# Cross-attention on one core: weighted context with the context as the moving operand, turned back by PE

## What is computed

```python
q = jnp.einsum('bte,ef->btf', emb, Wq) + bq
k = jnp.einsum('bml,le->bme', latent, Wk) + bk
v = jnp.einsum('bml,le->bme', latent, Wv) + bv
w = jnp.einsum('bte,bme->btm', q, k) * scale
w = jax.nn.softmax(w, axis=1)
pred = jnp.einsum('btm,bme->bte', w, v)
x = pred + emb
mu = jnp.mean(x, axis=-1, keepdims=True)
var = jnp.var(x, axis=-1, keepdims=True)
return (x - mu) * jax.lax.rsqrt(var + EPS) * gamma + beta
```

## Time and profile before

| | us |
|---|---|
| median of 3 runs (151.82 to 151.93) | 151.87 |
| the profiled execution | 151.6 |
| its span | 149.8 |

### The profile page before, as it was taken

The page is one execution under the profiler, slowest core; times in us unless marked ns, Lnnn a source line. Parts: engine busy times, 40 slices in busy tenths (PEclk is TensorE's granted clock), DMA queues, the critical chain, the costliest instruction groups (busy, mean ns, idle before and its releaser), DMA issues.

```text
span 149.8 us, 3112 instructions
## 1 busy us (share of the span) xinstructions
PE 138.9 (93%) x1070; PEld 130.7 (87%) x1070; DVE 119.8 (80%) x227; ACT 85.8 (57%) x292; POOL 87.5 (58%) x78
## 2 busy tenths in 40 slices
PE   7899999899899999999999999999999999999900
PEld 7789999798898989999998989899998989897700
DVE  0799989699777888779697978779697968777981
ACT  4468365289527937575573938475573938474410
POOL 0350049809032495866849494856749494859880
PEclk9999999999999999999999999999999999999996
DMA  4999659998065579889888989999888984653123
GB/s 136 296 352 418 275 154 285 377 293 322 25 209 198 193 285 334 288 267 306 265 263 305 267 321 280 322 257 335 263 260 284 285 308 122 241 190 114 55 69 95
DMA packets 11336, 37.14 MB, mean 248 GB/s; under 512 B 1422, under 2 KB 1934, under 8 KB 11322
## 3 DMA queue, kind: packets, MB, share of 16 engines
q1 hardware_dynamic: 9714, 34.50, 69.1%
q10 hardware_dynamic: 1608, 2.46, 4.6%
HBM read 33.68 MB, written 3.28 MB: 247 GB/s over the span
## 4 chain that ended last, share of the span: by engine, by line
PE 70%; DVE 14%; POOL 6%; DMA 3%; issue 2%; ACT 1%; SPq 1%; POOLq 1%; DVEq 0%
PE ps_U L372 27%; PE ps_S L358 26%; PE ps_Y L391 12%; DVE xu L624 6%; PE ps_U L333 3%; POOL result L810 3%; DMA wkT<-WkT 3%; DVE xT_lo L612 2%; POOL resid L800 2%; DVE wq_lo L598 2%; DVE wkq L604 1%; DVE W_lo L708 1%; PE ps_w L381 1%; POOL prob L790 1%; ACT xu_hi L483 1%
## 5 line engine op out<-in xcount | busy, mean ns | idle before, releaser
L494 ACT ACTIVATE expo<-scores,negmax 121x100 f32<-121x100 f32 x96 | 35.0, 366 | 26.6 <-DVE negmax L644 26.6
L358 PE MATMUL ps_S<-G,ctxT_in 128*121 128x100 f32 (+1 forms) x384 | 43.7, 270 | 0.6 <-DVE scores L640 0.6
L372 PEld LDWEIGHTS ps_U<-prob,ctx_in 121*128 121x128 f32 x360 | 42.4, 192 | 1.5
L358 PEld LDWEIGHTS ps_S<-G,ctxT_in 128*121 128x121 f32 (+1 forms) x384 | 41.9, 185 | 0.9 <-issue 0.9
L372 PE MATMUL ps_U<-prob,ctx_in 121*128 121x100 f32 x360 | 42.4, 274 | 0.0
L804 POOL TENSOR_TENSOR rstd<-vareps,neg_half 100x1 f32<-100x1 f32 x16 | 15.4, 960 | 27.5 <-DVE vareps L680 25.5
L790 POOL TENSOR_TENSOR prob<-expo,rinv 121x600 f32<-121x600 f32 x16 | 19.0, 1189 | 9.0 <-DVE rinv L651 9.0
L800 POOL TENSOR_TENSOR resid<-x_in,bvw 100x512 f32<-100x512 f32 x16 | 20.4, 1273 | 4.6 <-ACT bvw L511 4.4
L640 DVE TENSOR_TENSOR scores<-ps_S,c_rows 121x600 f32<-121x600 f32 x16 | 12.5, 782 | 13.2 <-issue 11.8
L657 DVE TENSOR_REDUCE probsum<-prob 121x100 f32<-121x600 f32 x16 | 19.8, 1239 | 1.0 <-POOL prob L790 0.6
L810 POOL TENSOR_TENSOR result<-scaled,beta_rows 100x512 f32<-100x512 f32 x15 | 19.3, 1291 | 0.0
(11 more groups left out here) (92 smaller groups left out, 184.1 us busy)
## 6 DMA issues: line engine op xcount, KB each, us to landing
ctx_in<-ctx SPq DMA_DIRECT2D x16, 768.0 KB, 6.4
ctxT_in<-ctxT SPq DMA_DIRECT2D x16, 722.0 KB, 6.6
xT_in<-xT SPq DMA_DIRECT2D x8, 400.0 KB, 5.9
x_in<-x SPq DMA_DIRECT2D x16, 200.0 KB
out<-result ACTq DMA_DIRECT2D x12, 200.0 KB
wqT<-WqT SPq DMA_DIRECT2D x4, 256.0 KB, 3.4
out<-result SPq DMA_DIRECT2D x3, 200.0 KB
wkT<-WkT SPq DMA_DIRECT2D x4, 128.0 KB, 3.9
```

What stands on the lines that cost most here:

```text
L358: last = nc.tensor.matmul(ps_scores(c)[0:rows(c), :], ctxT_in[:, q, l * M + c * MP:l * M + c * MP + rows(c)], G[:, l, bass.ds(b * T, T)], ...
L372: last = nc.tensor.matmul(ps_U[:, q, l * T:(l + 1) * T], ctx_in[0:rows(c), q, c, l * P:(l + 1) * P], prob[0:rows(c), q, c * T:(c + 1) * T] ...
L494: last = nc.scalar.activation(expo[0:MP, q, c * T:(c + 1) * T], scores[0:MP, q, c * T:(c + 1) * T], ACT.Exp, bias=negmax[0:MP, q, c:c + 1] ...
```

## The change

- `weighted_ctx` swaps its operands: `prob` of a chunk (100 columns) is stationary and the chunk's 256 context columns move. Six matmuls take the place of twelve, and the result has the query in the partition.
- Since the next step needs the context column there, ACT copies the result to `UT` (`take_UT`), and PE turns it with two transposes into `ps_c` (`turn_U`); `upper_U` and `lower_U` read `ps_c`.
- In a turn, the matmuls of the scores of batch b and of the weighted context of batch b-2 alternate: score half 0, weighted, score half 1, for each chunk. Both sets of waits stand ahead of the first matmul (`scores_and_weighted`).
- The values of batch b-3 follow that block, then the turning of batch b-2.
- `ctx_in` has three buffers; the order of SP's queue stays as it is. `centred` and `scaled` lie in the space of `wqT`.
- The turns of ACT, DVE and POOL are in another order, and the last batch is no longer split by halves. `identity` is made by POOL at the start.

The core of the diff:

```diff
-        ctx_in = sb("ctx_in", [P, 2, MC, L])
+        ctx_in = sb("ctx_in", [P, NC, MC, L])
...
+        identity = sb("identity", [T, T])
+        UT = sb("UT", [T, 2, L])
...
-            def next_ctx(b, q):
-                sp.wait_ge(U_done, b - 1)
-                load_ctx(b, q)
+            def next_ctx(b):
+                if b >= NC:
+                    sp.wait_ge(U_done, b - NC + 1)
+                load_ctx(b)
...
+            def before_weighted(b, q):
+                pe.wait_ge(ctx_loaded[b % NC], 16 * (b // NC) + 16)
+                pe.wait_ge(prob_set, b + 1)
+                if not first_two(b):
+                    pe.wait_ge(UT_set, b - 1)
+                else:
+                    pe.wait_ge(G_set, NG)
+
+            def weighted_chunk(b, q, c):
+                done = nc.tensor.matmul(ps_U[0:T, q, 0:L], prob[0:rows(c), q, c * T:(c + 1) * T],
+                                        ctx_in[0:rows(c), b % NC, c, :], start=(c == 0), stop=(c == MC - 1))
+                if c == MC - 1:
+                    done.then_inc(U_done, 1)
...
+            def scores_and_weighted(b, q, between):
+
+                before_scores(b, q)
+                before_weighted(b - 2, q)
+                for c in range(MC):
+                    score_chunk(b, q, c, 0)
+                    weighted_chunk(b - 2, q, c)
+                    score_chunk(b, q, c, 1)
+                    if c == 1 and between is not None:
+                        between()
+
+            def turn_U(b, q):
+                pe.wait_ge(UT_set, b + 1)
+                if b > 0:
+                    pe.wait_ge(Uhi_set, b)
+                    pe.wait_ge(Ulo_set, b)
                 else:
-                    pe.wait_ge(G_set, NG)
+                    pe.wait_ge(identity_set, 2)
+                    pe.wait_ge(c_set, NG)
                 for l in range(LC):
-                    for c in range(MC):
-                        last = nc.tensor.matmul(ps_U[:, q, l * T:(l + 1) * T],
-                                                ctx_in[0:rows(c), q, c, l * P:(l + 1) * P],
-                                                prob[0:rows(c), q, c * T:(c + 1) * T], start=(c == 0), stop=(c == MC - 1))
-                last.then_inc(U_done, 1)
+                    last = nc.tensor.transpose(ps_c[:, l * T:(l + 1) * T], UT[:, q, l * P:(l + 1) * P], identity[:, :])
+                last.then_inc(U_turned, 1)
...
             def turn(b, q):
-                if exists(b):
-                    scores_of(b, q)
-                if exists(b - 3):
-                    values(b - 3, 1 - q)
-                if exists(b - 2):
-                    weighted_ctx(b - 2, q)
-                    weight_sum(b - 2, q)
-
-
+                scores_and_weighted(b, q, None)
+                weight_sum(b - 2, q)
+                values(b - 3, 1 - q)
+                turn_U(b - 2, q)
...
-            turn(2, 0)
+            scores_of(2, 0)
             sum_shift(3)
+            weighted_ctx(0, 0)
+            weight_sum(0, 0)
+            scores_and_weighted(3, 1, lambda: turn_U(0, 0))
+            weight_sum(1, 1)
             pe.wait_ge(Wvhi_set, 1)
             pe.wait_ge(Wvlo_set, 1)
-            each_turn(turn, 3)
-
+            values(0, 0)
+            turn_U(1, 1)
+            each_turn(turn, 4)
             weighted_ctx(B - 2, 0)
             weight_sum(B - 2, 0)
             values(B - 3, 1)
+            turn_U(B - 2, 0)
+            weighted_ctx(B - 1, 1)
+            weight_sum(B - 1, 1)
             values(B - 2, 0)
-            weight_sum(B - 1, 1)
-
-
...
+            turn_U(B - 1, 1)
+            values(B - 1, 1)
...
+            def take_UT(b, q):
+                act.wait_ge(U_done, b + 1)
+                if not first_two(b):
+                    act.wait_ge(U_turned, b - 1)
+                nc.scalar.activation(UT[:, q, :], ps_U[0:T, q, 0:L], ACT.Copy).then_inc(UT_set, 1)
+
             def upper_U(b, q):
-                act.wait_ge(U_done, b + 1)
+                act.wait_ge(U_turned, b + 1)
                 if not first_two(b):
                     act.wait_ge(Y_done, b - 1)
-                nc.scalar.activation(U_hi[:, q, :], ps_U[:, q, 0:LC * T], ACT.Copy).then_inc(Uhi_set, 1)
+                nc.scalar.activation(U_hi[:, q, :], ps_c[:, 0:LC * T], ACT.Copy).then_inc(Uhi_set, 1)
...
             def turn(b, q):
-                if exists(b - 3):
-                    upper_U(b - 3, 1 - q)
-                    value_bias(b - 3, 1 - q)
+                take_UT(b - 2, q)
                 if exists(b - 4):
                     scale_rows(b - 4, q)
-                if exists(b):
-                    exponentials(b, q)
-                    if exists(b - 4):
-                        store(b - 4, q)
+                upper_U(b - 2, q)
+                exponentials(b, q)
+                value_bias(b - 2, q)
+                if exists(b - 4):
+                    store(b - 4, q)
...
+            take_UT(B - 2, 0)
             scale_rows(B - 4, 0)
+            value_bias(B - 2, 0)
             upper_U(B - 2, 0)
-            value_bias(B - 2, 0)
+            take_UT(B - 1, 1)
             value_bias(B - 1, 1)
...
-                scale_rows(B - 3 + l, 1 - l)
+            scale_rows(B - 3, 1)
+            upper_U(B - 1, 1)
+            scale_rows(B - 2, 0)
...
             def turn(b, q):
-                if exists(b - 1):
-                    normaliser(b - 1, 1 - q)
-                if exists(b - 3):
-                    lower_U(b - 3, 1 - q)
-                if exists(b):
-                    maxima(b, q)
+                maxima(b, q)
                 if exists(b - 3):
                     add_residual(b - 3, 1 - q)
+                lower_U(b - 2, q)
+                if exists(b - 3):
                     row_stats(b - 3, 1 - q)
-                if exists(b - 1):
-                    chunk_sum(b - 1, 1 - q)
-                if exists(b - 3):
                     centre(b - 3, 1 - q)
+                chunk_sum(b - 1, 1 - q)
+                normaliser(b, q)
...
             def turn(b, q):
                 if exists(b - 4):
-                    inverse_deviation(b - 4, q)
+                    finish(b - 4, q)
                 if exists(b - 3):
-                    residual(b - 3, 1 - q)
-                if exists(b - 4):
-                    finish(b - 4, q)
-                if exists(b - 1):
-                    probabilities(b - 1, 1 - q)
+                    inverse_deviation(b - 3, 1 - q)
+                probabilities(b, q)
+                residual(b - 2, q)
...
-            each_turn(turn, 2)
-            inverse_deviation(B - 4, 0)
-            residual(B - 3, 1)
-            probabilities(B - 1, 1)
-            residual(B - 2, 0)
+            probabilities(1, 1)
+            probabilities(2, 0)
+            residual(0, 0)
+            each_turn(turn, 3)
             finish(B - 4, 0)
             inverse_deviation(B - 3, 1)
+            residual(B - 2, 0)
+            finish(B - 3, 1)
             residual(B - 1, 1)
             inverse_deviation(B - 2, 0)
-            finish(B - 3, 1)
             finish(B - 2, 0)
             inverse_deviation(B - 1, 1)
...
```

More of the change, by code:

```diff
@@ L135, in xattn @@
         ctxT_loaded = [sem(f"ctxT_loaded{q}") for q in range(2)]
-        ctx_loaded = [sem(f"ctx_loaded{q}") for q in range(2)]
+        ctx_loaded = [sem(f"ctx_loaded{q}") for q in range(NC)]
         x_loaded = [sem(f"x_loaded{q}") for q in range(2)]
@@ L355, in scores_of, with score_chunk @@
                     pe.wait_ge(scores_zeroed, 1)
+            def score_chunk(b, q, c, l):
+                done = nc.tensor.matmul(ps_scores(c)[0:rows(c), :],
+                                        ctxT_in[:, q, l * M + c * MP:l * M + c * MP + rows(c)],
+                                        G[:, l, bass.ds(b * T, T)], start=(l == 0), stop=(l == LC - 1))
+                if c == MC - 1 and l == LC - 1:
+                    done.then_inc(S_done, 1)
+            def before_weighted(b, q):
[5 more added lines that the diff above has]
+                    pe.wait_ge(G_set, NG)
@@ L356, in scores_of @@
+            def weighted_chunk(b, q, c):
[3 more added lines that the diff above has]
+                    done.then_inc(U_done, 1)
+            def scores_of(b, q):
+                before_scores(b, q)
                 for c in range(MC):
                     for l in range(LC):
-                        last = nc.tensor.matmul(ps_scores(c)[0:rows(c), :],
-                                                ctxT_in[:, q, l * M + c * MP:l * M + c * MP + rows(c)],
-                                                G[:, l, bass.ds(b * T, T)], start=(l == 0), stop=(l == LC - 1))
@@ L361, in scores_of @@
[L361 removed]
+                        score_chunk(b, q, c, l)
             def weighted_ctx(b, q):
[L364 to L369 removed]
+                before_weighted(b, q)
+                for c in range(MC):
+                    weighted_chunk(b, q, c)
@@ L430, in _ @@
             values(B - 3, 1)
+            turn_U(B - 2, 0)
```

(50 more changed lines are left out.)

56 lines of the change are left out of this document (25 added, 31 removed).

## The result

The changed kernel takes 161.5 us (median of 4 runs, three of them between 161.32 and 161.60; the fourth, 168.99, was slower at a lower granted clock, 0.951, and is left out of the ratio, as is one run of 160.81 in an experiment below) against 151.9 for the kernel before, run beside it. The ratio is 1.063, 95% interval 1.061 to 1.065. The prediction said 161.8, within 157.3 to 165.0, and slower.

What follows compares the result with a forecast made beforehand. The prediction took PE's gapless stream, with loads just in time, to bound the kernel. Start 1.06, middle 4.5 and end 4.5 sum to 10.1 us on 151.6, so 161.7; it said 161.8, range 157.3 to 165.

Steps and rivals of the forecast that it cites:

- Bound of the kernel before: Turns 4 to 15: PE's stream without a gap, 6.76 us a turn, provided the loads still come in time.
- A weighted record 225 ns: Weighted context on PE: each record with 256 moving columns takes 225 ns, bounded between 116 and 284.
- the middle term: Eleven steps from turn 4 to 15: 0.19 us for two, nine at 0.46, in all 4.5 us.
- Loads behind `resid` late: SP's queue: x and both context loads go out together after resid, landing 7.9 us later; 7.22 us a turn; chance 0.60.
- the three-turn sum: Middle turns: 8.65 us to the issue, 7.9 to the landing, 5.11 for the block, 21.66 over three turns.
- Rival "loads in time": Middle turns: only PE's stream and the end count, 157.5 to 159.0 us; chance 0.27.
- Rival "faster": Weighted records on PE: 256 columns move in 116 ns, PE's turn 5.6 us, total 148.9; chance 0.06.
- "Load not hidden": Weighted records on PE also pay the next load's 87 to 105 ns: 176 us; chance 0.06, shared with two-pass transposes.
- Start: Before turn 4's scores: shift wait of about 0.6 us, batch 0's weighted context alone and batch 3's block; 1.06 us later.
- End: From turn 15 on: waits for probsum and resid of batch 14, last batch unsplit; 4.5 us longer.

Runs made afterwards that it cites:

- x last: Changed kernel with SP's loop issuing context, then transposed context, then x, so no context load stands behind the wait for resid: 157.73 us, ratio 1.038.
- the mended kernel: Changed kernel with x's load last, DVE's probsum of batch 14 earlier and POOL's residuals of 14 and 15 ahead at the end: 156.48 us, ratio 1.030.
- the run on the start: Weighted context and weight sum of batch 0 moved ahead of the last shift sum, against the 156.48 us kernel with its end reordered: 156.42 us, ratio 1.029.
- two buffers: Changed kernel with two buffers for the context in place of three: 161.33 us, ratio 1.062 against the kernel before.
- the scores first: Changed kernel with a turn's scores first and its weighted context behind them, not alternating: 158.92 us, ratio 1.046 against the kernel before.
- the first try at the end: Changed kernel with probsum 14 ahead of batch 12's statistics, resid 14 ahead of rstd 13, upper U(15) ahead of scaling 13: 162.12 us, ratio 1.066.
- two buffers with x last: Changed kernel with two context buffers in place of three and x's load last in SP's turn: 157.94 us, ratio 1.039 against the kernel before.

## Why the prediction was right, step by step

- **Bound of the kernel before: right.** It was PE's stream with loads just in time. The order of the loads alone moved 3.8 us.
- **A weighted record 225 ns: slightly high.** 216 measured; the 213 that the prediction gave from the Trainium skill ("FP8 and Floating Point Precision", TensorE Precision Notes: four passes for float32) was nearer. The block took 5.03 for 5.11, two transposes 0.18 (93.93 to 94.11) for 0.22, one record each. PE's turn is thus 6.76, not 6.90, and the 1.5 us of PE in the middle term didn't exist. That is one mis-sized term.
- **Loads behind `resid` late: right in mechanism, wrong in shape and size.** Residual 8.4 us after the block's end (85.50 to 93.88) for 8.65. Landing for 7.9: the eleven contexts that turns 5 to 15 use came 6.7 to 8.6 us after x, seven of them 7.4 or less (72.66 to 80.07 is one). The earlier trace rows says that nothing else was in flight; in fact the transposed context issued at 41.24 landed only at 45.25, so its 4.2 us are nearly, but not quite, those of a load alone (4.1 at 125.40). But the waits don't come evenly, 0.46 a turn: one turn has 2.0 us of the 3.9, six have 0.1 or less. With the times read here the three-turn sum gives (8.4 + 7.4 + 5.03)/3 = 6.94, nearly PE's own pace, and with a landing of 8.55 it gives 7.33; a load that is now and then slow pays in full, and the turns between give nothing back. The middle's 4.5 was 3.0 of waits and 1.5 of PE; measured are 3.9 and 0. Its nearness to 3.9 is partly luck, two errors that cancel.
- **Rival "loads in time": what the runs with x last show.** 157.73 lies in the 157.5 to 159.0 that it was given. The rival's physics was sound, but SP's order excluded it.
- **Rival "faster": excluded** by 216 ns a record, where it needed under 160. **"Load not hidden": excluded** by the 0.84 us chunk, which is two records of 216, three of 105 and one of 90 with nothing left over.
- **Start: +1.38 for 1.06.** Of it 0.42 is there before anything that the change touches (scores of batch 1 at 30.21 against 29.79, the first weights having landed 0.36 us later), so the change's part is 0.96. In the trace of the mended kernel the same scores start at 29.89, so the 0.42 is not a cost of the change. The wait for the shift was 0.67, for 0.6. That this wait could be won back by order alone fell with the run on the start.
- **End: +4.8 for 4.5, and by the steps named.** `probsum` of 14 held the weight sum for 1.08 (predicted 1.3), the residual of 14 held y(14) for 1.74, y(15) came 21.9 us after turn 15's start (predicted 21.0), but what follows it took 7.3 us for the 7.8 of the prediction, so here too two misses partly cancel. The mended order wins 1.25 us of it. What the lost split has in it is not shown. Of the mended kernel's remaining 4.6 us against the one before, about 1 is the start and 3.5 the end (27.9 us from turn 15 against 24.4). No run separates its parts; its trace shows PE waiting 0.60, 0.59 and 1.58 us there.

So the change loses because it wins nothing on PE: twelve records of 216 ns stand in for 24 of 111, the block with its alternation is 0.24 us shorter than scores and weighted context were (5.03 for 5.27), and the transposes take 0.18 of that. What remains is what came with it: 3.8 us by SP's queue, about 1 at the start, and the rest in the drain, of which one order explains 1.25 and the other part stays open.

## What to carry to other kernels

Price both sides of an operand swap as slots, the larger of own moving time and next weight load, before counting the instructions saved: half as many records of twice the length are no gain. A load's issue is only as early as the latest wait ahead of it in its queue, so put the load with the latest condition last in the turn before adding buffers. An operation moved off one wait is worth what the next engine's order allows: y(15) gained only when the residual behind the moved work was moved too, and the values among the weighted records only as long as DVE's idle time took the delay.

## What the runs showed of the hardware

- One float32 matmul of 256 moving columns is two records of 216 ns with 100-column loads hidden behind them; a float32 transpose of 100x128 is one record, and two of them take 0.18 us of PE's stream.
- The moving side of a record and the next load overlap record by record: 233 + 111 + 90 ns for a float32r value and the two records of a weighted matmul, with no cost for changing between float32r and float32 that the 0.43 us shows.
- Three loads issued within 0.7 to 1.1 us of each other landed 6.7 to 8.6 us after the first, where one nearly alone took 4.2. The context of batch 9 was slow in four traces with the changed kernel's order of SP's queue: 7.8 us after its own issue in the changed kernel, 8.1 with two buffers, 8.0 with the scores first, 7.8 in the first try at the end; the kernel before took 6.0. One issue on SP's queue took 1.80 us instead of 0.31 to 0.48 (94.62), ahead of the longest wait. I had expected neither that nor that a pace set by such loads would be uneven by 2 us in one turn. The long issue isn't needed for it: with two buffers the same issue took 0.43 us, and in the first try at the end the context of batch 6 landed 7.8 us after an issue of 0.43. Why these loads land late stays open.
- TensorE's granted clock fell behind some waits of PE and not behind others: 0.53 for 3.53 us behind 2.07 us (two buffers) and 0.50 for 2.6 us behind 2.44 us (two buffers with x last), but 1.00 behind 1.76 and 2.43 us in the changed kernel and behind 1.86 us in the first try at the end. With two buffers the wait of 2.07 us made its turn 4.0 us longer.
